# Half of a softmax's row sum moved from TensorE to VectorE: the two halves of a unit's exponentials added in place

## The reference, cut to what matters

```
q = layernorm(x) @ wq + bq
offsets = pointwise(gelu(depthwise_conv(q as image, 7x7, stride 2)))
interp = bilinear sample of x at 256 positions set by the offsets
k, v = interp @ wv + bv
attn = softmax(heads(q @ mq_w + mq_b) . heads(k @ mk_w + mk_b))   # 8 heads, 1024 x 256
z = (attn . heads(v @ mv_w + mv_b)) @ mo_w + mo_b + x
out = gelu(layernorm(z) @ mlp_w + mlp_b) + z
y = out + sigma * (softmax(theta(out) . pool(phi(out))) . pool(g(out))) @ w_o + ...
```

## Time and profile before

| | us |
|---|---|
| median of 3 runs | 514.73 (513.17 to 515.65) |
| the profiled execution | 512.36 |
| its span, first to last instruction | 510.6 |
| TensorE busy | 454.9 (89%) |
| VectorE busy | 286.2 (56%) |
| ScalarE busy | 211.6 (41%) |
| GpSimd busy | 120.1 (24%) |

### The profile page before, as it was taken

One profiled execution on the slowest core, in us unless ns is written; L12 is line 12 of the kernel. 1 busy time (PEld: TensorE's weight loads), 2 busy tenths in 40 slices (PEclk: granted clock), 3 DMA queues, 4 the chain that ended last, 5 costly groups with the idle time before them and its releaser, 6 DMA issues.

```text
span 510.6 us, 9319 instructions
## 1 busy us (share of the span) xinstructions
PE 454.9 (89%) x3743; PEld 318.8 (62%) x3743; DVE 286.2 (56%) x609; ACT 211.6 (41%) x338; POOL 120.1 (24%) x163
## 2 busy tenths in 40 slices
PE   6788979988989999989899999989899897888956
PEld 5657756645567576656686666656767564665735
DVE  4518446846673367667754345567546647625433
ACT  1122212545346045655333336745173664662230
POOL 5420301167003001681002003761030030100000
PEclk9999989989999999999999999999999998999978
DMA  7298866581947930293157801472226200000202
GB/s 211 76 168 171 163 101 126 85 169 65 137 69 99 233 54 3 85 124 64 42 101 103 164 3 46 90 111 27 83 42 86 83 3 2 1 2 2 82 2 83
DMA packets 30489, 42.90 MB, mean 84 GB/s; under 512 B 6075, under 2 KB 21230, under 8 KB 30446
## 3 DMA queue, kind: packets, MB, share of 16 engines
q1 hardware_dynamic: 23598, 34.82, 37.4%
q0 software_dynamic: 3584, 4.50, 3.8%
q10 hardware_dynamic: 3264, 2.99, 2.9%
HBM read 16.16 MB, written 4.19 MB: 40 GB/s over the span
## 4 chain that ended last, share of the span: by engine, by line
PE 57%; DVE 13%; DMA 10%; POOL 7%; issue 5%; ACT 5%; SPq 1%; ACTq 0%; DVEq 0%; POOLq 0%
PE ps_d L759 8%; PE ps_d L884 5%; PE ps_d L861 5%; PE ps_d L961 5%; PE ps_d L747 4%; PE ps_s L808 4%; DMA xa<-in_x_dram 4%; PE ps_v L850 4%; DMA corners<-in_x_dram,row_of 3%; PE ps_v L844 3%; PE ps_t L827 3%; PE ps_d L779 3%; POOL samp L1937 3%; DVE mx L1613 3%; PE ps_d L903 2%
## 5 line engine op out<-in xcount | busy, mean ns | idle before, releaser
L1226 ACT ACTIVATE prob<-ps_t 128x1024 f32<-128x1024 f32 x64 | 65.4, 1021 | 95.8 <-PE ps_t L827 92.2
L1613 DVE TENSOR_REDUCE mx<-ps_s 128x4 f32<-128x1024 f32 x64 | 78.2, 1222 | 24.1 <-PE ps_s L808 23.2
L1909 POOL DMA_DIRECT2D q_st<-mx_t x64 | 34.0, 532 | 244.0 <-ACT mx_t L1218 226.0
L759 PE MATMUL ps_d<-cstack,conv_w 128*32 128x256 f32 x1024 | 59.0, 380 | 3.4 <-issue 1.8
L808 PE MATMUL ps_s<-k_st,q_st 96*128 96x256 f32 x256 | 49.9, 317 | 8.2 <-DVE mx L1613 7.1
L759 PEld LDWEIGHTS ps_d<-cstack,conv_w 128*32 128x32 f32 x1024 | 36.3, 108 | 23.9 <-issue 6.2
L808 PEld LDWEIGHTS ps_s<-k_st,q_st 96*128 96x128 f32 x256 | 35.9, 191 | 20.5 <-DVE mx L1613 12.6
L827 PE MATMUL ps_t<-q_st,k_st 98*128 98x256 f32 x256 | 42.6, 289 | 6.2 <-ACT zt L1285 3.0
L827 PEld LDWEIGHTS ps_t<-q_st,k_st 98*128 98x128 f32 x256 | 35.5, 192 | 8.9 <-issue 5.1
L1627 DVE TENSOR_TENSOR att<-ps_v,rden 128x256 f32<-128x256 f32 x32 | 13.6, 424 | 43.2 <-ACT rden L1237 43.2
L844 PE MATMUL ps_v<-prob,vh 128*32 128x256 f32 x512 | 35.1, 392 | 1.5 <-DVE att L1627 1.5
(11 more groups left out here) (178 smaller groups left out, 744.7 us busy)
## 6 DMA issues: line engine op xcount, KB each, us to landing
q_st<-q_parts SPq DMA_DIRECT2D x42, 256.0 KB, 5.6
xa<-in_x_dram SPq DMA_DIRECT2D x8, 512.0 KB, 9.6
z_all<-in_x_dram SPq DMA_DIRECT2D x8, 512.0 KB, 7.9
out_dram<-z_all SPq DMA_DIRECT2D x8, 512.0 KB, 2.6
cstack<-qpad SPq DMA_DIRECT2D x22, 180.5 KB, 5.7
k_st<-cstack SPq DMA_DIRECT2D x22, 128.0 KB, 4.2
q_st<-z_all SPq DMA_DIRECT2D x6, 256.0 KB, 5.7
cstack<-att SPq DMA_DIRECT2D x6, 180.5 KB, 9.8
```

The lines of the kernel that those rows point to most:

```text
L759: ins = pe.matmul(ps[32 * k:32 * k + 32, 0, :], conv_w[:, cb * 4 + k, y, x, :], cstack[:, cb, k, y:y + HG_, x:x + WG_], start=n == 0, stop ...
L1226: drain(act.activation(prob[:, u % 2, 2 * pr:2 * pr + 2].rearrange("p h m s -> p (h m) s"), ps_t[:], ACT.Exp), t_ring, "t", b, u, pr)
L1613: drain(dve.tensor_reduce(mx[:, u % 2, half, :], ps_s[:], AX.X, ALU.max), s_ring, "s", b, u, half)
```

## The change

From unit 5 of image 0, which falls in slot 0 of image 1, to unit 4 of image 3, which falls in slot 7 of image 3, VectorE adds the second half of the unit's exponentials to the first, in place, after the mix has read both, and TensorE multiplies `ones` by the first half alone. Two semaphores order this: the last matmul of the mix counts `mixed_done`, for which the add waits; the add counts `halves_done`, for which the sums wait. The first five units and the last three (in the tail) stay as they were. In VectorE's slot the add stands behind the first maximum, the corner weights and the normalised rows, and before all the rest.

```diff
+def halves_before(b, u):
+    return UNITS * b + u + 1 - (UNITS - 3)
...
-            def values_mixed(b, u):
+            def values_mixed(b, u, added=False):
...
-                        pe.matmul(ps_v[32 * h:32 * h + 32, 0, :], vh[:, mt, hh * HD:(hh + 1) * HD],
-                                  prob[:, u % 2, h, mt, :], start=mt == 0, stop=mt == 1)
-
-            def values_summed(b, u):
-                for mt in range(2):
+                        ins = pe.matmul(ps_v[32 * h:32 * h + 32, 0, :], vh[:, mt, hh * HD:(hh + 1) * HD],
+                                        prob[:, u % 2, h, mt, :], start=mt == 0, stop=mt == 1)
+                if added:
+                    ins.then_inc(mixed_done, 1)
+
+            def values_summed(b, u, added=False):
+
+                if added:
+                    pe.wait_ge(halves_done, halves_before(b, u))
+                for mt in range(1 if added else 2):
                     for h in range(HQ):
                         ins = pe.matmul(ps_v[32 * h:32 * h + 32, 1, :], ones[:], prob[:, u % 2, h, mt, :],
-                                        start=mt == 0, stop=mt == 1)
+                                        start=mt == 0, stop=added or mt == 1)
...
-                    values_mixed(*unit_of(b, s, 3))
+                    values_mixed(*unit_of(b, s, 3), added=b > 0)
...
-                    values_summed(*unit_of(b, s, 3))
+                    values_summed(*unit_of(b, s, 3), added=b > 0)
...
+            def add_halves(b, u):
+                dve.wait_ge(mixed_done, halves_before(b, u))
+                part = prob[:, u % 2]
+                dve.tensor_tensor(part[:, :, 0, :], part[:, :, 0, :], part[:, :, 1, :], ALU.add).then_inc(halves_done, 1)
...
                 if s == 0 and post:
                     residual_norm(m, 0)
+                if b:
+                    add_halves(*unit_of(b, s, 3))
                 if in_front(b, s, "qimg0") and b > 1:
                     row_shift(n, range(NJ, NT))
```

More of the change, by code:

```diff
@@ L386, in build @@
         max_in = [signal(f"max_in{k}", UNITS, 16) for k in range(2)]
+        mixed_done = sem("mixed_done")
+        halves_done = sem("halves_done")
         den_log = signal("den_log", UNITS)
```

## The result

The changed kernel takes 525.58 us (median of 5 runs, 523.52 to 527.25), the kernel before 515.28 (5 runs): ratio 1.0204, interval 1.0172 to 1.0235. It is 10.3 us slower; 513.7 was forecast and the range ended at 519.0. The profiled execution took 524.56 us.

The account below looks back on a forecast made before the run. TensorE, 89% busy, was taken to bound the kernel, with its waits deciding what comes back. Gain -7.1, delays +3.7 and GpSimd's hold +2.4 make -1.0 us: median 514.73 to 513.7, range 510.6 to 519.0.

Parts of the forecast that it names:

- The gain of a slot: Summing one half instead of two was to save TensorE 0.50 us in each of 24 units.
- the 7.1 us: Total gain: twelve slots at 0.50, slot 7 of images 1 and 2 at 0.4 each, 0.3 in image 3.
- the copy in slot 2: Images 1 and 2: TensorE's 0.94 us wait for VectorE's query image copy was to grow to some 2.1 us.
- slot 4 of image 1: The add delays the copy of the first queries; forecast as nothing gained, nothing lost.
- slot 5 costs: Images 1 and 2: sums wait 0.75 us for the add and save 0.50, so 0.25 us later.
- slot 0 of image 1 (I had 0.3): The add delays the query image copy past when TensorE wants its bank: 0.3 us lost.
- GpSimd's hold: Slots 5 and 6, images 1 and 2: each add lengthens GpSimd's chain 0.6 us, 2.4 us in all.
- the upper bound of 1.14: Most that one add was taken to hold GpSimd: a whole VectorE pitch, 2.28 us an image.
- the clock: TensorE's clock falls before the keys, slot 6 of images 1 and 2, if GpSimd is fully held: 1.7 us each.
- twice 1.14 = 2.3 us: Slot 2 of images 1 and 2: the add delays VectorE's query image copy, with nothing to hide it.
- another 1.14 us: Slot 0 of image 2: the add delays the result rows, for which TensorE already waits.
- The slower rival: Slot 6, images 1 and 2: both adds hold GpSimd and TensorE's clock falls, 519.3 us; chance 0.16.

Follow-up runs that it names:

- sum_only: Kernel before with one half summed in the 24 slots and no add on VectorE (denominators lack a half): 514.2 us, ratio 0.9954.
- quiet_and_0_2: Kernel before with adds in ten slots expected to hide them, plus slots 0 and 2 of images 1 and 2: 520.5 us, ratio 1.0097.
- one_input: Changed kernel with a one-input maximum over 1024 values replacing the add in slots 5 and 6 of images 1 and 2: 518.5 us, ratio 1.0068.
- add_only: Changed kernel with the add in all 24 slots, but TensorE still sums both halves: 522.9 us, ratio 1.0167.
- busy_gaps: Changed kernel plus unread matmuls filling TensorE's idle time in slots 2 and 6 of images 1 and 2: 522.2 us, ratio 1.0150.
- sum_only_busy: sum_only plus unread matmuls in slot 6 of images 1 and 2: 513.8 us, ratio 0.9871.
- the ten quiet slots: Kernel before with the change only in slots 1, 3 (image 1), 1, 3, 4 (image 2), 2 to 5, 7 (image 3): 514.2 us, ratio 0.9953.
- quiet_seven: Kernel before with the change in the ten quiet slots and in slot 7 of images 1 and 2: 514.9 us, ratio 0.9980.
- its twin: quiet_seven plus unread matmuls in slot 6 of images 1, 2 and 3: 512.1 us, ratio 0.9935.

## Why the prediction was wrong

*Bounds, counts and sizes.* Right: 320 records, 24 adds, a median of 1215 ns for an add against 1.22 us, a pitch of 1.13 us, and waits for the halves in slot 5 of images 1 and 2 and nowhere else, at 0.8 us. The gain of a slot was 0.50 by half of the earlier trace rows; it is 0.41 to 0.54, mostly 0.43, and 0.13 in slot 4 of image 3. With the clock's falls left out (slot 2 of images 1 and 2 and slot 7 of image 3 taken at 0.43) the 7.1 us are about 6.2.

*The delays.* Found in the right places, at the right size: the copy in slot 2 waits 2.1 us as forecast, slot 0 of image 2 is 1.14 us longer, slot 4 of image 1 is 0.00, slot 5 costs 0.44 and 0.41 (I had 0.25). Slot 2 of image 1 lost 0.13 us and not 0.64, since the convolution behind it became 0.57 shorter. For slot 0 of image 1 (I had 0.3) the profiles scatter too much to tell.

*GpSimd's hold.* Forecast 0.6 us an add, measured 0.84 and 0.80: 1.65 us an image for 1.2, so 0.9 us too little in two images. In image 2 the lengths are the same to 0.01 us. The chain is 13.75 us for a forecast of 13.3. The Trainium skill, "SBUF — State Buffer" (Who interferes with whom), says that the second of the two waits for the first; the rows agree, 0.84 of 0.97 us that the first add still had to run, and VectorE itself waited 0.44 us when it was second. The truth lies between the 0.6 that I took and the upper bound of 1.14, nearer the 0.6.

*The step that failed is the clock.* I weighed it in one place, the keys, on one condition, that both adds hold GpSimd for nearly their whole length, and gave that 0.16. The runs show three things in its place. It needs no hold: removing sums alone makes it fall there (`sum_only`). It follows the order delays too: "twice 1.14 = 2.3 us" and "another 1.14 us" were costed as bare waits, and in `quiet_and_0_2` two of them took 2.82 and 2.26. And it is not a matter of a wait's size alone: waits of 1.08 and 0.48 us came with a fall in image 1 of `one_input` and the same without one in image 2, and 0.78 and 1.53 us came without one in `add_only`. How much it is in all can be read from runs of one unchanged kernel: over the 95 runs of the kernel before in the four groups, time falls by 3.9 us for each 0.01 of mean granted clock (correlation -0.83, mean 0.974 at 515.5 us; 3.6 to 4.5 us in the single groups). The changed kernel's five runs have a mean of 0.950. An estimate from these: 2.4 x 3.9 = 9.4 us of its 10.3. What is left, about 1 us, is what the other terms of my sum make when the sizes above are put in: -1.0 for the forecast, 0.9 less gain, 0.9 more hold, together 0.8. A slope over runs is no experiment. `busy_gaps` and `sum_only_busy` show the clock's part in slot 6 by intervention, and the 12.7 us of longer records point the same way; slot by slot the profile places some 6 us, 3.4 in slot 6 of images 1 and 2, 1.7 in slot 2 of image 2 (2.31 for 0.64) and 1.0 in slot 7 of image 3. That the clock makes nine tenths of the loss is an estimate and not shown. The slower rival, 519.3 us, named the right mechanism and place for two falls, at 1.7 us each (measured 1.5 and 1.9), with hold as its condition; it had neither the fall in slot 2 of image 2 nor the longer one in slot 7 of image 3.

*Open.* Why a fall follows one wait and not an equal one; whether GpSimd is held by the second read or by the write; and what the pause in the convolution of slot 2 waits for, which takes 1.0 to 1.2 us of the 3.6 that the ten quiet slots gain and may be the reason why the ratio shows 2.4. That more of the saved time is lost to the clock elsewhere is read from two profiles only: slot 7 of image 3 is 0.50 us longer in `quiet_seven` and 1.90 shorter in its twin, whose products make slot 6 1.05 longer.

## What to carry to other kernels

Before costing time taken off an engine that is 89% busy, list its waits: work removed ahead of a wait does not shorten the end, it lengthens the idle time, and on TensorE that can be paid for a second time in slower matmuls. Look for pauses without a recorded cause too, since they can swallow saved time in the same way. Cost every wait that the change makes longer with and without a fall of the clock behind it, and compare mean granted clocks of several runs before trusting a sum of slots from one profile. In this kernel an in-place add of two SBUF tiles was cheapest where GpSimd was at rest.

## What the hardware showed that I had not expected

- A VectorE maximum of 1024 values beside GpSimd's multiplies and adds costs GpSimd nothing (0.93, 2.47 us); an add of the same length costs 0.84 and 0.80.
- Matmuls without a reader in the idle time of slot 6, 1.56 and 1.46 us of them, make the eight records of the keys behind 1.99 us long instead of 3.39.
- One unchanged kernel on one core has runs from 509.4 to 520.3 us in one group of 28, and the granted clock goes with them (correlation -0.91).
- The same two waits, 1.08 and 0.48 us, have the clock fall behind them in one image and not in the next of one execution: eight records take 2.95 us and 1.97.
- Five kernels with fewer sums ahead of it have a pause of 1.0 to 1.2 us between two matmuls of one convolution, at a granted clock of 1.00, for which the profile names no cause; the two profiles of the kernel before have at most 0.18 us there.
- The first use of a transferred tile in slot 0 of image 1 waited 2.16 us in one profile and 3.67 in another of the same kernel; with the slow stretch behind it this is 3.15 us of a slot.
